# Context attention of a decoder kernel: rotated queries and keys turned by DMA transfers instead of by TensorE

## The reference

```python
def _L0_xattn_ref(draft_hidden, context_hidden, Wq, Wk, Wv, Wo, ...):
    H, KVH, HD = (16, 4, 128)
    q = (draft_hidden @ Wq.T).reshape(bsz, draft_len, H, HD)
    q = _rms_norm(q, q_norm_w).transpose(0, 2, 1, 3)
    kv_in = jnp.concatenate([context_hidden, draft_hidden], axis=1)
    k = (kv_in @ Wk.T).reshape(bsz, total_len, KVH, HD)
    v = (kv_in @ Wv.T).reshape(bsz, total_len, KVH, HD).transpose(0, 2, 1, 3)
    k = _rms_norm(k, k_norm_w).transpose(0, 2, 1, 3)
    q = _rope(q, draft_position_ids)
    k = _rope(k, full_position_ids)
    ...
    scores = jnp.einsum('bhqd,bhkd->bhqk', q, k) * SCALE
    probs = jax.nn.softmax(scores, axis=-1)
    attn = jnp.einsum('bhqk,bhkd->bhqd', probs, v)
    return attn.transpose(0, 2, 1, 3).reshape(bsz, draft_len, H * HD) @ Wo.T
```

## Time and profile before

| | |
|---|---|
| median of 3 runs | 3007.12 us (2999.63 to 3008.91) |
| profiled execution: device time | 3004.53 us |
| profiled execution: span | 3002.7 us |
| TensorE clock granted, mean | 0.969 of full speed |
| PE, DVE, ACT, POOL busy | 91%, 65%, 52%, 40% of the span |
| DMA queue of the kernel | 120.00 MB, 12.3% of 16 engines |

### The profile page before, as it was taken

How to read it: one execution, slowest core, us unless ns; L and a number is a source line. 1 busy time by engine, 2 the same in 40 slices (tenths; PEclk the granted TensorE clock), 3 DMA queues, 4 the chain that set the end, 5 groups by cost and what they waited for, 6 DMA issues and landing times. The chain is left out here.

```text
span 3002.7 us, 49266 instructions
## 1 busy us (share of the span) xinstructions
PE 2727.9 (91%) x17011; PEld 1595.3 (53%) x17276; DVE 1958.4 (65%) x3681; ACT 1574.4 (52%) x3629; POOL 1204.2 (40%) x1238
## 2 busy tenths in 40 slices
PE   6789896899999999959976998998889999999998
PEld 4677672555555555524434665666654444444443
DVE  5778896878787888767656788887463232322335
ACT  7999983655555555464417777676432221222121
POOL 3889885745454545224333111111142212222121
PEclk8999997999999999989997999999989999999999
DMA  4111103100000000040012000000021111111211
GB/s 161 40 54 48 43 33 120 43 5 8 4 7 4 7 4 4 1 168 1 1 50 74 19 19 18 14 16 19 12 90 65 45 50 63 63 63 32 65 32 67
DMA packets 50541, 122.53 MB, mean 41 GB/s; under 512 B 7042, under 2 KB 11522, under 8 KB 48163
## 3 DMA queue, kind: packets, MB, share of 16 engines
q1 hardware_dynamic: 50338, 120.00, 12.3%
HBM read 111.25 MB, written 4.52 MB: 39 GB/s over the span
## 5 line engine op out<-in xcount | busy, mean ns | idle before, releaser
L2060 POOL TENSOR_TENSOR s_state<-s_state,s_ct 128x512 f32<-128x512 f32 x256 | 326.8, 1302 | 82.0 <-DVE s_state L2235 79.6
L2235 DVE TENSOR_TENSOR_SCAN s_state<-s_decay,s_psd 128x512 f32<-128x512 f32 x256 | 301.8, 1208 | 68.3 <-PE s_psd L2380 34.7
L1044 DVE TENSOR_TENSOR m_prod<-m_bank,m_gated 128x512 f32<-128x512 f32 x88 | 60.8, 691 | 437.6 <-ACT m_gated L853 437.6
L779 POOL TENSOR_TENSOR m_aTl<-m_prod,m_aTh 128x512 bf16<-128x512 f32 x88 | 101.8, 1157 | 584.0 <-ACT m_aTh L855 584.0
L853 ACT ACTIVATE m_gated<-m_bank 128x512 f32<-128x512 f32 x88 | 52.5, 597 | 437.3 <-PE m_bank L1166 437.3
L1156 PE MATMUL m_bank<-m_xTl,m_wh 128*128 128x512 bf16 x704 | 267.8, 380 | 3.1 <-ACT m_wh L819 1.0
L1155 PE MATMUL m_bank<-m_xTh,m_wh 128*128 128x512 bf16 x671 | 255.5, 381 | 2.4 <-DVE m_prod L1044 2.4
L2380 PE MATMUL s_psd<-ident,s_v 128*128 128x128 f32 x1024 | 166.0, 287 | 41.8 <-DVE s_state L2235 21.1
L2136 ACT ACTIVATE s_decay<-s_dt,s_nega 128x508 f32<-128x508 f32 x256 | 181.6, 710 | 20.4 <-DVE s_state L2235 20.3
L2149 ACT ACTIVATE s_v<-s_uT,s_bT 128x512 f32<-128x512 f32 x256 | 182.1, 712 | 0.8 <-PE s_psd L2380 0.7
L2380 PEld LDWEIGHTS s_psd<-ident,s_v 128*128 128x128 f32 x1024 | 123.1, 147 | 88.6 <-ACT s_v L2149 47.1
(11 more groups left out here) (516 smaller groups left out, 8070.2 us busy)
## 6 DMA issues: line engine op xcount, KB each, us to landing
s_ct<-ssm_bc SPq DMA_DIRECT2D x64, 256.0 KB, 3.2
m_scale<-moe_scale SPq DMA_DIRECT2D x64, 256.0 KB, 3.2
m_stage<-in_moe_w_dram SPq DMA_DIRECT2D x16, 768.0 KB, 5.0
m_stage<-in_moe_w_dram SPq DMA_DIRECT2D x8, 864.0 KB, 7.8
X<-in_x_dram SPq DMA_DIRECT2D x4, 1024.0 KB, 12.2
a_cf<-in_ctxT_dram SPq DMA_DIRECT2D x16, 256.0 KB, 2.7
a_wstage<-in_xa_wq_dram SPq DMA_DIRECT2D x8, 512.0 KB, 3.6
a_wstage<-in_xa_wo_dram SPq DMA_DIRECT2D x8, 512.0 KB, 4.0
```

The lines of the kernel that those rows point to most:

```text
L2060: pool.tensor_tensor(h, h, ct[t % 4][:, s * P:(s + 1) * P].unsqueeze(1).broadcast_to([P, KB, P]), ALU.mult).then_inc(weighted, 1)
L2235: dve.tensor_tensor_scan(state[i % RING][:, :], decay[t % 2][:, s, :, :].rearrange("p m t -> p (m t)"), ps_d[i % 2][:, :], 0.0, ALU.mult, ...
```

## The change

The rotated chunk is no longer turned by PE. It is split while it is still in rows, into a buffer `a_rotp` of 128 x 2 x 512 bf16 (one for even, one for odd chunks): the high part by ACT from `a_rot` in SBUF, the low part by POOL (DVE did it before). Then one DMA transposition on SP's queue turns both parts, eight blocks of 128x128 bf16 (256 KB), and writes them to `a_kT` or `a_qT`. The high part of chunk c waits until the transfer of chunk c-2 has left the buffer; the scores wait for the transfers instead of for DVE. The probabilities are still turned by PE, and their two banks are now theirs alone.

```diff
+            def turn_chunks(n, g, j):
+                if g == 0:
+                    return
+                for c in (2 * g - 2, 2 * g - 1):
+                    r = c % 2
+                    sp.wait_ge(t_low.sem, t_low.at(n, c + 1))
+                    if c < QC:
+                        if late(n, 2):
+                            sp.wait_ge(scored.sem, scored.at(n - 2))
+                        out = kT[j][:, :, :, c, :].rearrange("p a h t -> p (a h) t")
+                    else:
+                        if late(n, 1):
+                            sp.wait_ge(scored.sem, scored.at(n - 1, c - QC + 1))
+                        out = qT[:, c - QC, :, :, :].rearrange("p a h t -> p (a h) t")
+                    sp.dma_start(out, rotp[r][:, :, :].rearrange("p a n -> p (a n)"), transpose=True).then_inc(t_done[r].sem, 16)
@@ SP, a turn
+            def turn(s, p, start=None, last=False, last_x=False):
+                for g in range(4):
+                    if g == 0 and not last_x:
+                        context(s + 2)
+                    if start == 0 and g:
+                        wl.sync(sp, wlow, first_wo + 2 * g + 1, min(first_wo + 2 * g + 3, nchunks))
+                    if not last:
+                        turn_chunks(s + 1, g, 1 - p)
@@ POOL
+            def turned_low(n, c):
+                pool.wait_ge(t_high.sem, t_high.at(n, c + 1))
+                pool.tensor_tensor(rotp[c % 2][:, 1, :], rot[c % 2][:, :], rotp[c % 2][:, 0, :], ALU.subtract).then_inc(t_low.sem, 1)
...
                 for g in range(4):
+                    if g and not last:
+                        turned_low(s + 1, 2 * g - 2)
                     if not last_x:
                         if g == 0:
                             x_copy(s + 2)
-                        if g == 1:
                             angles(s + 2)
...
+                    if g and not last:
+                        turned_low(s + 1, 2 * g - 1)
                     if not last:
                         front(s + 1, g, 1 - p)
@@ ACT
-            def turned_high(n, g, j):
...
+            def turned_high(n, c):
+                r = c % 2
+                act.wait_ge(roped.sem, roped.at(n, 2 * c + 2))
+                if c >= 2 or late(n, 1):
+                    act.wait_ge(t_done[r].sem, t_done[r].at(n, 16 * (c // 2)) if c >= 2 else t_done[r].at(n - 1))
+                act.activation(rotp[r][:, 0, :], rot[r][:, :], ACT.Copy).then_inc(t_high.sem, 1)
...
+                    if g and not last:
+                        turned_high(s + 1, 2 * g - 2)
                     exponentials(s, g, p)
...
-                        turned_high(s + 1, g, 1 - p)
+                        if g:
+                            turned_high(s + 1, 2 * g - 1)
                         chunk(s + 1, 2 * g + 1, 1 - p)
@@ DVE: turned_low is gone, and the products of a chunk wait for POOL's low part
-                    dve.wait_ge(turned.sem, turned.at(n, c - 1) if c >= 2 else turned.at(n - 1, 5 + c))
+                    dve.wait_ge(t_low.sem, t_low.at(n, c - 1) if c >= 2 else t_low.at(n - 1, 5 + c))
@@ PE: turn_chunks is gone; scores and turn_probs wait for other semaphores
-                pe.wait_ge(t_low.sem, t_low.at(s, QC + g + 1))
+                r = g % 2
+                if g == 0:
+                    pe.wait_ge(t_done[1].sem, t_done[1].at(s, 16))
+                pe.wait_ge(t_done[r].sem, t_done[r].at(s, 16 * (g // 2 + 2)))
...
                 pe.wait_ge(normed.sem, normed.at(s, g + 1))
-                pe.wait_ge(t_low.sem, low_of)
+                if g or late(s, 1):
+                    pe.wait_ge(p_low.sem, p_low.at(s, 2 * g) if g else p_low.at(s - 1))
```

More of the change, by code:

```diff
@@ L136, with __init__ @@
     STEPS = 5
-    def __init__(self, fr, st, tag, eps=1e-5):
+    def __init__(self, fr, st, tag, eps=1e-5, r=None):
         self.fr, self.eps = fr, eps
-        self.r = fr.sb(f"{tag}_ln_r", [P, D], F32, st)
+        self.r = fr.sb(f"{tag}_ln_r", [P, D], F32, st) if r is None else r
         self.stats = fr.sb(f"{tag}_ln_stats", [P, 6], F32, st)
@@ L1252, in stage_xattn @@
         woh, wol = (fr.sb(f"a_wo{n}", [P, 16, D], BF16, st) for n in "hl")
-        ln = LayerNorm(fr, st, "a")
+        wstage = [fr.sb(f"a_wstage{j}", [P, 1024], F32, st)[:, :] for j in range(3)]
+        ln = LayerNorm(fr, st, "a", r=wstage[2][:, 0:D])
         xs = fr.sb("a_xs", [P, D], F32, st)
@@ L1278, in stage_xattn @@
         qscale = [fr.sb(f"a_qscale{j}", [P, 16], F32, st) for j in range(2)]
-        qTh, qTl = (fr.sb(f"a_qT{n}", [P, 16, P], BF16, st) for n in "hl")
-        kTh = [fr.sb(f"a_kTh{j}", [P, KV, 2 * P], BF16, st) for j in range(2)]
-        kTl = [fr.sb(f"a_kTl{j}", [P, KV, 2 * P], BF16, st) for j in range(2)]
+        qT = fr.sb("a_qT", [P, KV, 2, GH, P], BF16, st)
+        rotp = [fr.sb(f"a_rotp{j}", [P, 2, 512], BF16, st) for j in range(2)]
+        kT = [fr.sb(f"a_kT{j}", [P, 2, KV, 2, P], BF16, st) for j in range(2)]
         vh = [fr.sb(f"a_vh{j}", [P, 2, 512], BF16, st) for j in range(2)]
@@ L1330, in stage_xattn @@
         v_low = Count(fr, "a_vlow", 2)
-        turned = Count(fr, "a_turned", 6)
+        t_done = [Count(fr, f"a_tdone{r}", 48) for r in range(2)]
         t_high = Count(fr, "a_thigh", 6)
@@ L1376, in _ @@
             wl.sync(sp, wlow, 4, first_wo)
[L1377 to L1380, removed]
+            turn_chunks(0, 1, 0)
+            wl.sync(sp, wlow, first_wo, first_wo + 3)
+            turn_chunks(0, 2, 0)
+            turn_chunks(0, 3, 0)
+            turn(0, 0, start=0)
+            for s in range(1, SEQS - 2):
+                turn(s, s % 2)
+            turn(SEQS - 2, 0, last_x=True)
+            turn(SEQS - 1, 1, last=True, last_x=True)
         @block.gpsimd
@@ L1469, in _ @@
             c_low_part(1, 1)
-            for g in range(3):
+            for g in range(4):
+                if g:
+                    turned_low(0, 2 * g - 2)
+                    turned_low(0, 2 * g - 1)
                 if g == 1:
@@ L1748, in turn_x @@
                 mm.then_inc(x_turned.sem, 1)
[L1750 to L1760, removed]
             def chunk(n, c, j):
@@ L1826, in turn @@
                     if g:
-                        turn_probs(s, g - 1, t_low.at(s) if g == 1 or last else t_low.at(s + 1, 2 * g - 2))
+                        turn_probs(s, g - 1)
                     elif start != 0:
-                        turn_probs(s - 1, 3, t_low.at(s))
+                        turn_probs(s - 1, 3)
                     if not last:
```

46 lines of the change are left out of this document (9 added, 37 removed).

## The result

The changed kernel takes 2982.72 us (median of 3 runs, 2981.92 to 2984.60) against 3007.12; the ratio of the two is 0.9926, with a 95% interval from 0.9913 to 0.9939. So it is faster, by 24 us or 0.7%, where I forecast 43. Its profiled execution took 2982.72 us as well, with a span of 2980.9: 21.8 less than before.

| kernel | state space | context att. | its start | turn | end | FFN | pair att. | experts |
|---|---|---|---|---|---|---|---|---|
| before | 464.6 | 836.7 | 126.2 | 48.74 | 125.6 | 264.0 | 618.9 | 818.4 |
| after | 463.9 | 800.8 | 134.9 | 45.44 | 120.6 | 265.4 | 633.2 | 817.5 |

A forecast was written before the change was run, and what follows sets the result against it. PE was taken to bound the steady context attention. Gains of 37.0 (transpositions), 3 (turn 0) and 3 (waits) sum to 43 us, from 3004.5 to 2961.5, stated as 2964 on the runs' scale; range 2946 to 2996 (8 in 10).

The forecast's parts named there:

- PE's transpositions: Context attention turns: eight float32 transpositions leave PE's list in three quarters, 2.64 us a turn, 37.0 us over turns 1 to 14.
- PE's waits: Context attention turns: PE's remaining waits for `a_pTl` shrink by 0.2 us a turn, 3 us in all.
- VectorE has room to 46.2 us: Context attention: after the change DVE needs 40.9 us of a 46.2 us turn, so PE still ends last.
- rival 2: No change: POOL's new operations delay DVE, which takes over from PE as bound; 3013 us, in part 2984; chance 0.14.
- ScalarE's high parts ahead of the exponentials: Context attention turn: ACT's high parts standing before the exponentials delay them by 0.6 us a turn, between 0 and 1.9.
- The transfers: Each 256 KB DMA transposition on SP's queue takes 5 us and costs nothing beyond SP's time.
- rival 3: Landings between 8.5 and 14 us hold ACT in every quarter; the gain shrinks to some 10 us, 2995; chance 0.04.
- the bound of 7.7 us: If the transfers don't overlap, six must fit in a turn of 46.2 us, 7.7 us each.
- upper bounds of 7.5 and 15 us: One DMA transposition as 1024 pieces at 0.117 us over 16 engines: 7.5 us, or 15 if writing doubles it.
- the estimate of 10.5 us: One DMA transposition as eight blocks in a row at 1309 ns each; a turn of 63 us, some 3217 us.
- Turn 0 and the prologue: Start of the context attention: turn 0 gains 3 us (0 to 8.3), the prologue 0, with 4 either way.
- main case: The change works with PE still the bound: 2964 us, own range 2950 to 2978; chance 0.68.

## Why the prediction was half right

- **PE's transpositions, 2.64 us a turn:** right. Put back, they cost 2.73.
- **PE's waits, 0.2 us a turn:** too little, it was 0.57, inside my bounds (0.75). `a_pTl` fell from 12.9 us in 20 waits to 6.2 in 22, and only 0.47 of 100 us are left of PE's idle time. That VectorE's list ends earlier in each quarter, and that the step undervalued this, fits these rows, but nothing tested it.
- **VectorE has room to 46.2 us (rival 2 from 5.9 us of delays on):** the sum was wrong, the side right. By it, six low parts more would need 40.9 + 3.8 = 44.7 us and hide under PE. They made the turn 47.48, at 87% busy: of 3.8 us 2.0 showed, so by this estimate VectorE had some 1.8 us of room at those places and not 45.4 - 40.9 = 4.5. The likely reason, not tested by itself, is that VectorE's part of each quarter is a chain through ScalarE and back, which a sum of busy time and one wait misses. What kept the change fast is the move to GpSimd.
- **GpSimd:** right: 1157 ns each, 71.08% busy. VectorE's shift takes no longer in the mean, 466 ns before and 397 after (650 to 1150 us), though its median rose from 174 to 415: the delays have become more and shorter.
- **ScalarE's high parts ahead of the exponentials, 0.6 us:** borne out; VectorE's wait for the exponentials rose from 51.0 / 10.3 = 5.0 us a turn to 59.0 / 11 = 5.4, without a cost that the turn shows.
- **The transfers:** right that they hide; 3.1 us, not 5, and they overlap: with two more a chunk the turn doesn't change, and no landing took over 5.8 us, so rival 3 didn't arise. Where the chain of a chunk is made longer than a sixth of the turn, it does set the turn, as the bound of 7.7 us says: 9.1 us each gave 57.10. My upper bounds of 7.5 and 15 us priced a piece by the queue's mean. The count was right: (151714 - 50338) / 96 = 1056 pieces of about 250 B. But the queue's share rose from 12.3 to 17.1% only, or (0.171 x 2980.9 - 0.123 x 3002.7) x 16 / 101376 = 0.022 us each. On the rule of the Trainium skill that I weighed ("VectorE: DVE Perf Modes", "The three transpose paths", 1309 ns a block): eight blocks in 3.1 us are not eight times that, and the estimate of 10.5 us fell. What the Trainium skill's "Advanced Engine Details and Errata", "DMA Advanced Topics", says of X-Bar Transpose, as fast as regular DMAs, agrees: 3.1 against 2.8 us for the plain 256 KB. What stands near 1309 ns here is SyncE's time to issue one, 1232 ns, and it covers all eight blocks.
- **Turn 0 and the prologue, +3 and 0 (with 4 either way):** wrong, -8.7. I counted busy time (six operations each way) and took it that none is on the path. In the start GpSimd is busy for 77.41 of 99 us and its list is a chain with ScalarE: each low part waits for a high part that stands behind splits of weights still on their way, and VectorE waits for the low part.
- **The other stages, 0:** not named at all, and the largest miss: 14.3 us. The change took 36 instructions from VectorE's list ahead of the pair attention (its loop begins as the 2375th instead of the 2411th), and in that place the loop of 258 instructions stands at both of its jumps back; that it lies across a piece border at both ends is the reading that one shift supports.

Sum: 39.6 + 5.0 - 8.7 - 14.3 + 0.2 for the rest = 21.8 us. Without the stall the change gives about 36 us (2970.67 with 3 memsets); the forecast of 43 was the right mechanism with the start 12 us too good and the turns 4.6 too poor. The time measured, 2982.7, lies above the main case's own 2950 to 2978. It is inside the range of 2946 to 2996 only by the room given to the main case's far ends and to rivals 2 and 3, and what filled it is none of them but the stall in the pair attention: that the range held is luck. (A reading that changes nothing: PE's digits in the earlier trace rows are 9 from the ninth slice on, not from the eighth.)

## What to carry to other kernels

An engine that is 78% busy is not free by 22% (8% of a turn more on VectorE made the turn 2 us longer): test what it bears by putting the work back on it, and look at the chain within one quarter, not at the sum over a turn. When work leaves or enters an engine's list, look at the profile of the stages behind it, whose code is unchanged: if a loop there gets a stand of some 5 us "issue" once in a pass and the engine's instruction queue moves packets during it, shift the list by a few cheap instructions before judging the change. And count a prologue as a chain of its own, not with the steady state's slack.

## What was not expected of the hardware

A loop on VectorE loads its instructions anew in each pass or not at all, by its length and place: 16 loads in 360 us of a loop of 282 instructions, none with 270, 17 with the same 270 moved by 19. In the context attention such loads mostly hide (up to 0.4 us a turn), but in the pair attention VectorE stood 5.1 to 5.4 us, a shift by 3 removed it, and the other kernel got it when its loop was put exactly 128 instructions behind. A DMA transposition of 128x1024 in bf16 (256 KB) between SBUF tiles lands in 3.1 us, nearly the same with three in flight (3.3), and costs SyncE 1.23 us to issue, against 0.53 for the plain load of 256 KB in the same loop and 0.34 in the pair attention.
